# Nine groups, a second copy of the middle stream's sum, a narrow condition product, and layer 2's scores as four row strips

## The chip, the cores and the metric

The kernel runs on one core of one Trainium2 chip. The metric is the device time of one execution in microseconds (us), as the median of several runs. Nothing is split over cores: one core computes all 32 batches.

## The reference

Four transformer-like layers are applied one after the other to `x` (32 batches, 128 tokens, 128 features, float32), with a condition vector `cond` per batch:

```
layer 0: x += g * attn(mod(ln(x)));  16 heads of 64;  x += g * gelu_mlp(mod(ln(x)))
layer 1: x += proj(attn(film(rms(x)))), 1 head of 128;  x += gelu_mlp(film(rms(x)))
layer 2: x += g * attn(mod(ln(x)));  16 heads of 8;  x += g * gelu_mlp(mod(ln(x)))
layer 3: q_exp = where(row_sum(x) == 0, 0, cond)            # per token
         self  = concat(x, q_exp) @ W_self.T + b_self
         for d in 0, 1: A = adj (or transposed)[:, :, :20]  # 11 labels for each edge
             scores = self.Wq . self[:20].Wk + labels' bias, masked; 16 heads of 8, softmax over 20
             out   += heads' outputs
         x = x + relu(out + self)
```

Two facts matter below. In layer 2 each head has only 8 features, so a score product uses few of TensorE's 128 rows. In layer 3 `W_self` is applied to a concatenation whose second half is either zero or the batch's condition vector, the same for all tokens.

## The kernel before

The 32 batches are worked through in 8 groups of 4 (`G = 4`, so a group has T = 512 token columns, one PSUM bank of float32). Each group passes four **streams** of steps: *front* (layer 0's attention, 8 pairs of heads), *mid* (layer 0's MLP and layer 1), *back* (layer 2) and *end* (layer 3). Letters name a stream of one group: A to H the fronts, I to P the mids, Q to X the backs, a to h the ends. `STEPS` (lines 68 to 158) lists each stream's steps; `ORDERS` (line 181 on) holds, for each of the four engines PE, DVE, ACT and POOL, one string of 1357 letters that was written out by a planner: each letter takes the next step of its stream. Every engine works strictly through its own string and waits on semaphores inside the steps, so a wait on PE holds up everything that follows in PE's string. Groups overlap only as the strings interleave them: in the PE string the mid of group g runs beside the front of g+1, the back beside the front of g+2, the end beside the front of g+3. After the last letter H (front of the last group) there remain P, W, X, f, g and h, and the last 18 letters are h alone. A front has 76 steps, a mid 25, a back 51, an end 18.

`Plan` (line 302) deals the eight PSUM banks: it walks through PE's string and gives each result that begins at a step the bank that was freed longest ago. `order_pairs` (line 242) lists which steps of neighbouring groups must stay in order because they share a buffer. One of them is `y2` of a back before `down (1, 1)` of the next mid: both use the single buffer `x1`, which carries layer 1's result to layer 2.

The steps that the change touches:

- `S2` of a back (PE line 1122): layer 2's scores. A batch has 4 strips of 32 rows (`strip(u)`, 4 heads each) and so 4 units u; the unit's bank gets 4 heads x 128 keys. The moving operand `km` is the keys, zero but for one head in each part. Step k takes two units, 2k and 2k+1, that is two strips and two banks; a batch has two such steps. DVE takes the row maximum (line 1442), ACT the exponentials with their sums (932), PE transposes (1138), ACT copies (938), and `V2` multiplies with the values (1148), one step for a batch, in four column strips.
- `sum3`, `self3` of an end (PE lines 1173 to 1177): `sum3` multiplies x3T with ones; DVE makes `qx` of it (1528: the condition where the sum isn't zero); `self3` adds two products, one of x3T and one of `qx`, and DVE adds the bias (1369) to get `sT`.
- `adj` of an end (PE line 1167, DVE 1508): transposes the edge sums that came by the other direction and builds mask and bias.
- `edges` of a back: 12 pieces of the adjacency, converted on ACT (927), multiplied on POOL (786) and summed twice on DVE (1437, 1438); 4 of 20 edges for all 128 tokens, 8 of 16 edges on 80 partitions.

Float32 products appear in the trace as two MATMUL records each, transposes as one.

Of the kernel before, what the change touches and what calls it, by code (L numbers as in the profile page):

```python
# [12 lines left out]
D = 128  # L13
B = 32
G = 4
NG = B // G
# [38 lines left out]
NJ = 2 * G  # L55
# [59 lines left out]
def back_steps():  # L115
    steps = norm_steps(4) + [Step("kq2", 0, ["k2", "q2"], ["k2", "q2"]), Step("v2", 0, ["v2"], ["v2"])]
    for s in range(2 * G + 1):
        for what, lag in (("S2", 0), ("T2", 1), ("T2'", 1), ("E2", 0)):
            w = s - lag
            if not 0 <= w < 2 * G:  # L120
                continue
            begins, ends = {"S2": ([("A", 2 * w), ("A", 2 * w + 1)], [("A", 2 * w)]),
# [11 lines left out]
def end_steps():  # L134
    steps = [Step("adj", 0, ["adj"], ["adj"]), Step("sum3", 0, ["sum3"], ["sum3"]),
             Step("self3", 0, ["self3"], ["self3"]), Step("qk3", 0, ["q3_0", "q3_1", "k3"], ["q3_0", "q3_1", "k3"])]
    for s in range(NU3 + 5):
        begins, ends = [], []
        if s < 2:
            begins.append(f"vb_{s}")  # L140
            ends.append(f"vb_{s}")
        if s in (S4 + 4, NU3 + 4):
            begins.append(f"a3_{s // S4 - 2}")
            ends.append(f"a3_{s // S4 - 2}")
        if 0 <= s - 4 < NU3:
            begins.append(("T3", s - 4))
            ends.append(("T3", s - 4))
        if s < NU3:
# [9 lines left out]
FRONTS, MIDS, BACKS, ENDS = "ABCDEFGH", "IJKLMNOP", "QRSTUVWX", "abcdefgh"  # L158
STEPS = {}
for _g in range(NG):  # L160
    STEPS.update({FRONTS[_g]: front_steps(_g + 1 < NG), MIDS[_g]: mid_steps(), BACKS[_g]: back_steps(), ENDS[_g]: end_steps()})


NPIECES = 12
PIECES = [(0, e, 20) for e in range(0, G * NK3, 20)] + [(1, e, 16) for e in range(0, D, 16)]
EDGE_EVERY = 3


def edge_slot(i):

    return i // EDGE_EVERY - 1 if i % EDGE_EVERY == 0 and i >= EDGE_EVERY else None

EDGE_LAST = EDGE_EVERY * (NPIECES + 2)

# [7 lines left out]
            "AAAAAAAAAAAAAAAAAAAAAAAAAAAAAAAAAAAAAAAAAAAAAAAAAAAAAAAAAAAAAAAAAAABBAAAAAAAAAIBIBBBBBIBBBBBBIBBIBBI"  # L184
            "IBBBIIBBBBBBBBBIBIBIIBIBIBBBBBBBIBBIBBBIIIBBBBBBBBBBBBIBBBIBIBBIBBIBBCCBBBBCCBBCBCQCCBCCQJJCCCCCJCQC"
            "CJJQCCQCQCQJQJQQQQCJQJCQCCQJCCCQCQCCCQQQJQCCCCCQQJQCJCQCQQJCCCQQJCJQCQJQCQCJCQQCCCQQQCCQCJJCQJCQCCCC"
            "QJQQJCCCQCCCJJQCCQCCCQCCQCDCQQDDDDRaDRRDDaRRDaKRRKDaKRRaKaKRKRDRRDKDRRaDDDDRDDDKDDRDRRRKDDRDRRDaDDDR"
            "DaRDDKRKDDDaDKRRDRKRRKDDKRDDDRaDDKDDDRDDDaRKDDKDRRKDDDKDRDRDKDRDaRDDDaDRDKRDKDDDDRKaRDDRRaKRDRDaRREa"
            "EELSELESbEESbESSbSESLSEbSLSLbSSELEbSLESSEEbEEEESELSEEESESESSLEEEEbSELSEESEbSESEELEESbLESEESSLLLSEESS"
            "bEEEEELEEESEbLSESLLESEEESSSEbELEESbLEEEEEEESLLSESbESSEbLELESEbSESESSFbTTMFFFcTMFcTTFFMFcFFTcTTMcMTTT"  # L190
            "TFFFMMTTTcFcFMTFFMFFFTFTTFMFFTTFFcFFTFFFTFcFTTFFTMFFFTTcTFTMMTMMTFFFFTcFFMFFcTFMTFMTFFTMFFFFTFFFFFFT"
            "cFFMTFFMFcTFMTMcTTcTFFFFMFcTMTFFTFTFTTGUGcUGGGGdGdUGNUUGNdUNUdUUNNdUdNUUUUGGNGdUUGGGNUGGGNGUGGNGUGUG"
            "UUGGUGdGGGUGdNGGUGUdNUUGGUUGGNNGGNGUUGdNGUGGNdGUGUGUGGGNGGUGGUUGGUGGNGNGdUGGGGNdUGGGNNUGGdUdUUGGNdUG"
            "GNUGUUUHHdVHGHVVeHVHVeHOOHVeVVVOeVOHOeVHHeHVHHHOVVOHHHeVHHHVVHHeOVVVVOVHeVeVVVOOVVHeOVeVOHeOOHHVHHVH"
            "HVHHeHOVHVHHHHVeVOHHOHVeHVVeHOVOHHHVHHOHHHVHVVOOeHHHHVVOVHHVHHHOHVVHHfWHHHHHfWHWfHWWfPWPWWPffPPWWWfP"
            "WPWWWPPPWWfWWPWWfWPfWPWPfWWfWPPWPWWWPWWfWWPfWWPfPWWWfWfWPWPWWfWPWPWWWWgXXXgXXXXXgXgXXXXgXgXXXXgXXXXX"
            "gXgXXXXXXXXgXXXXXggXXXgXXggXXgXXXgXXXXghhhhhhhhhhhhhhhhhh"),
        "DVE": (
            "AAAAAAAAAAAAAAAAAAAAAAAAAAAAAAAAAAAAAAAAAAAAAAAAAAAAAAAAAAAAAAAAAABAAAAABAAAAAIBBBBIBBIBBBBBBIIBBIBB"
# [1453 lines left out]
```

## Time and profile before

| | |
|---|---|
| median of 3 runs | 1184.86 us (1183.1 to 1186.69) |
| the profiled execution | 1181.46 us |
| its span in the trace | 1179.7 us |
| PE (TensorE) busy | 1085.0 us, 92% of the span, 8411 matmul records |
| DVE (VectorE) busy | 881.7 us, 75% |
| ACT (ScalarE) busy | 770.1 us, 65% |
| POOL (GpSimd) busy | 435.8 us, 37% |
| mean granted TensorE clock | 0.965 of full speed |

```profile
## 2 busy tenths in 40 slices
PE   5898999999999999999999999999989988778675
PEld 4565765776577656676667756766567755546434
DVE  2465767786899687996799788996887678858645
ACT  0655567984788547874789548974678628837712
```

Each digit is the busy share of one fortieth of the span (29.5 us), in tenths; 9 is 90% or more. PEld is TensorE's weight loading, which overlaps the products. In the rows below, a busy time is the time in which at least one instruction of the group ran, a mean is that of one instruction with its latency, and an idle time before a group says whom its engine waited for.

### The profile page before, as it was taken

The numbers are of one execution on the slowest core, as the hardware profiler recorded it, in microseconds if no ns is written. First come the engines' busy times: TensorE is split into PE (matmuls) and PEld (weight loads), VectorE is DVE, ScalarE is ACT, GpSimd is POOL, SyncE is SP. The second block draws the span as 40 slices with busy tenths as digits, with TensorE's granted clock in tenths as the row PEclk, the third lists the DMA queues.
The fourth block names the chain that finished last, engine by engine and source line by source line (L and its number), as shares of the span: only waits on it lengthen the run. The fifth ranks groups of instructions, "written<-read, shape, count | busy, mean of one in ns | idle before, by whom it ended". The sixth has DMA issues, their size and how long they took to land.

```text
span 1179.7 us, 24111 instructions
## 1 busy us (share of the span) xinstructions
PE 1085.0 (92%) x8411; PEld 734.9 (62%) x8411; DVE 881.7 (75%) x2510; ACT 770.1 (65%) x2888; POOL 435.8 (37%) x599
## 2 busy tenths in 40 slices
PE   5898999999999999999999999999989988778675
PEld 4565765776577656676667756766567755546434
DVE  2465767786899687996799788996887678858645
ACT  0655567984788547874789548974678628837712
POOL 1231323431454323542355324541344234515313
PEclk9999999999999989999999999999989999988885
DMA  8000000001000100001000100001000100010000
GB/s 259 2 9 1 11 10 1 10 11 32 1 11 11 32 10 9 2 11 41 1 11 3 39 9 11 2 2 40 1 10 2 41 1 1 2 40 1 1 9 10
DMA packets 21822, 20.98 MB, mean 18 GB/s; under 512 B 1143, under 2 KB 20296, under 8 KB 21448
## 3 DMA queue, kind: packets, MB, share of 16 engines
q1 hardware_dynamic: 18536, 15.26, 4.6%
q10 hardware_dynamic: 3168, 4.19, 1.2%
q8 instruction: 69, 1.13, 0.4%
q14 instruction: 49, 0.40, 0.1%
HBM read 17.35 MB, written 2.10 MB: 16 GB/s over the span
## 4 chain that ended last, share of the span: by engine, by line
PE 68%; DVE 19%; ACT 5%; POOL 4%; issue 3%; DMA 1%; POOLq 0%; DVEq 0%; ACTq 0%
PE bank L1002 11%; PE bank L1021 7%; PE bank L1009 7%; PE bank L1026 5%; PE bank L1047 5%; PE bank L1072 5%; PE bank L1062 5%; PE bank L1056 4%; PE bank L1130 4%; PE bank L1138 3%; PE bank L996 3%; PE bank L1148 2%; PE bank L1220 2%; PE bank L1209 2%; ACT prob_space L932 2%
## 5 line engine op out<-in xcount | busy, mean ns | idle before, releaser
L756 POOL TENSOR_TENSOR fprobs<-fprobs,frinv 128x512 f32<-128x512 f32 x128 | 132.7, 1041 | 249.2 <-DVE frinv L1315 248.3
L932 ACT ACTIVATE prob_space<-bank,negmax 128x128 f32<-128x128 f32 x512 | 181.4, 385 | 34.1 <-DVE negmax L1442 33.9
L868 ACT ACTIVATE fprobs<-bank,fnegmax 128x128 f32<-128x128 f32 x512 | 181.1, 388 | 31.3 <-DVE fnegmax L1310 31.1
L1002 PE MATMUL bank<-fhT,w_qkv 128*128 128x512 f32 x256 | 126.1, 615 | 1.5 <-DVE fv L1324 0.8
L729 POOL TENSOR_TENSOR rstd<-veps,half 128x4 f32<-128x4 f32 x40 | 40.5, 1014 | 208.6 <-DVE veps L1272 173.6
L868 ACT ACTIVATION_READ_ACCUMULATOR fprobs<-bank,fnegmax 128x1 f32 x512 | 116.7, 228 | 0.0
L932 ACT ACTIVATION_READ_ACCUMULATOR prob_space<-bank,negmax 128x1 f32 x512 | 115.7, 226 | 0.0
L1310 DVE TENSOR_REDUCE fnegmax<-bank 128x4 f32<-128x512 f32 x128 | 82.1, 682 | 40.3 <-PE bank L1047 39.8
L1442 DVE TENSOR_REDUCE negmax<-bank 128x4 f32<-128x512 f32 x128 | 82.2, 683 | 22.0 <-PE bank L1130 21.6
L874 ACT ACTIVATE fprobsT<-bank 128x512 f32<-128x512 f32 x128 | 74.5, 605 | 36.5 <-PE bank L1056 36.4
L879 ACT ACTIVATE fk<-bank 128x512 f32<-128x512 f32 x64 | 38.8, 607 | 82.0 <-PE bank L1002 82.0
L1138 PE MATMUL bank<-ident,prob_space 128*128 128x128 f32 x512 | 78.6, 287 | 6.0 <-ACT prob_space L932 5.6
L1056 PE MATMUL bank<-ident,fprobs 128*128 128x128 f32 x512 | 75.8, 279 | 7.6 <-POOL fprobs L756 7.0
L938 ACT ACTIVATE prob_space<-bank 128x512 f32<-128x512 f32 x128 | 76.4, 620 | 8.6 <-PE bank L1138 8.4
L1056 PEld LDWEIGHTS bank<-ident,fprobs 128*128 128x128 f32 x512 | 58.5, 142 | 36.2 <-issue 19.0
L1130 PE MATMUL bank<-km,qk 32*128 32x256 f32 x512 | 75.6, 422 | 3.5 <-POOL km L793 2.2
L1138 PEld LDWEIGHTS bank<-ident,prob_space 128*128 128x128 f32 x512 | 60.6, 147 | 27.3 <-issue 17.6
L1009 PEld LDWEIGHTS bank<-w_qkv,fhT 128*128 128x128 f32 x512 | 65.6, 194 | 19.0 <-issue 16.4
L838 POOL TENSOR_TENSOR p<-p,rinv 128x320 f32<-128x320 f32 x64 | 47.3, 740 | 75.8 <-DVE rinv L1548 75.8
L1047 PE MATMUL bank<-fk,fq 64*128 64x128 f32 x1024 | 74.4, 284 | 0.6 <-issue 0.2
L786 POOL TENSOR_TENSOR adjw<-adjf,labels 80x176 f32<-80x176 f32 (+1 forms) x96 | 53.6, 559 | 54.7 <-ACT adjf L927 54.7
L1047 PEld LDWEIGHTS bank<-fk,fq 64*128 64x128 f32 x1024 | 62.3, 187 | 17.7 <-issue 14.6
(193 smaller groups left out, 2503.6 us busy)
## 6 DMA issues: line engine op xcount, KB each, us to landing
adj<-in_mask_BxSxSx_ik SPq DMA_DIRECT2D x8, 440.0 KB
adj<-in_mask_BxSxSx_ik SPq DMA_DIRECT2D x32, 110.0 KB
x_norm<-in_x SPq DMA_DIRECT2D x8, 256.0 KB, 2.9
x_res<-in_x SPq DMA_DIRECT2D x8, 256.0 KB, 2.8
out<-x_out SPq DMA_DIRECT2D x8, 256.0 KB, 2.3
w_qkv<-in_L_cond_W_qkv ACTq DMA_DIRECT2D x1, 1536.0 KB, 6.9
prob_space<-in_w_mod SPq DMA_DIRECT2D x1, 1024.0 KB
w_up<-in_w_up ACTq DMA_DIRECT2D x1, 768.0 KB, 13.2
```

What stands on the lines that cost most here:

```text
L756: pool.tensor_tensor(p, p, wide(frinv[:, u, :], D), ALU.mult).then_inc(fnormed.sem, 1)
L868: ins = act.activation(fprobs[:, u % NP, b, :], P.bank(("S", u))[:, tok(b)], ACT.Exp, bias=fnegmax[:, u, b:b + 1], accum_out=frsum[:, u, b ...
L932: ins = act.activation(probs[:, u % NP, i, :], P.bank(("A", u))[:, tok(i)], ACT.Exp, bias=negmax[:, u, i:i + 1], accum_out=rsum[:, u, i:i ...
L1002: ins = pe.matmul(P.bank(result)[:, :], w, a, start=(i == 0), stop=(i == len(terms) - 1))
L1009: ins = pe.matmul(P.bank(result)[:, tok(b)], a[:, tok(b)], w, start=(i == 0), stop=(i == len(terms) - 1))
L1021: pe.matmul(P.bank(result)[:, :], w_up[:, l, tok(c)], part.hT[:, :], start=True, stop=True).then_inc(P.full_sem(result), 1)
L1047: ins = pe.matmul(P.bank(("S", 2 * c + r))[:, tok(b)], fq[rows, c % 2, tok(b)], fk[rows, c % 2, tok(b)], start=True, stop=True)
L1056: ins = pe.transpose(P.bank(("T", u))[:, tok(b)], fprobs[:, u % NP, b, :], ident[:, :])
L1130: ins = pe.matmul(P.bank(("A", u))[:, tok(2 * n, 2)], qk[strip(u), 0, tok(b)], flat(km[strip(u), b % 2, 2 * n:2 * n + 2, :]), start=True, ...
L1138: ins = pe.transpose(P.bank(("T", u))[:, tok(i)], probs[:, u % NP, i, :], ident[:, :])
L1310: dve.tensor_reduce(fnegmax[:, u, :], P.bank(("S", u))[:, :].rearrange("p (b k) -> p b k", b=G), AX.X, ALU.max, negate=True).then_inc(fmax ...
L1442: dve.tensor_reduce(negmax[:, u, :], P.bank(("A", u))[:, :].rearrange("p (i k) -> p i k", i=HS), AX.X, ALU.max, negate=True).then_inc(max2 ...
```

## The change

1. **Groups.** `SIZES = (2, 4, 4, 4, 4, 4, 4, 4, 2)` replaces 8 groups of 4. Every instruction that covered 512 columns covers `P.t = n * 128`; per-batch loops run over `P.n`; counts of semaphores are lists by group. The first and the last group have two batches. The adjacency comes in n + 8 pieces, in a small group one at every second step in place of every third.
2. **The orders.** All four strings are new (1483 letters each, fronts A to I, mids J to R, backs S to a, ends b to j). `x1` gets two copies, used in turn, and the order pair on it now ties the back of g to the mid of g+2. In the new PE string 128 letters stand ahead of the first mid (before: 78), the spans of neighbouring fronts overlap by 20 to 63 letters (before: by none to 17), after the last front's last step there remain a mid of 2 batches, backs of 4 and 2 and ends of 4, 4 and 2, and the last 14 letters are j alone, of 2 batches.
3. **The condition product.** `W_self`'s second half is multiplied with the group's condition columns themselves (n columns), in step `adj`; `qx` is then the product's column where the sum isn't zero, and is added on DVE.
4. **Layer 2's scores.** The even S2 step issues the products of all four strips into four banks; the odd one issues nothing on PE.

```diff
 G = 4
-NG = B // G
+SIZES = (2, 4, 4, 4, 4, 4, 4, 4, 2)
+NG = len(SIZES)
...
-            begins, ends = {"S2": ([("A", 2 * w), ("A", 2 * w + 1)], [("A", 2 * w)]),
+            begins, ends = {"S2": ([("A", 2 * w + j) for j in range(S4)] if w % 2 == 0 else [], [("A", 2 * w)]),
...
-PIECES = [(0, e, 20) for e in range(0, G * NK3, 20)] + [(1, e, 16) for e in range(0, D, 16)]
-EDGE_EVERY = 3
+PIECES = [[(0, e, 20) for e in range(0, n * NK3, 20)] + [(1, e, 16) for e in range(0, D, 16)] for n in SIZES]
+EDGE_EVERY = [3 if n == G else 2 for n in SIZES]
...
-        pairs.append((step_at(b, "y2"), step_at(m2, "down", (1, 1))))
+        if g + 2 < NG:
+            pairs.append((step_at(b, "y2"), step_at(MIDS[g + 2], "down", (1, 1))))
...
-        x1 = sb("x1", [D, G, D])
+        x1 = sb("x1", [D, 2, G, D])
...
                     elif what == "S2":
-                        b = k // 2
                         if k % 2 == 0:
+                            b, units = k // 2, range(2 * k, 2 * k + S4)
                             pe.wait_ge(*km_ready.nth(g, b))
-                        banks_free(P, drained=["q2"] if k == 0 else [], empty=[("A", u) for u in (2 * k, 2 * k + 1)])
-                        for n in range(2):
-                            for u in (2 * k, 2 * k + 1):
+                            banks_free(P, drained=["q2"] if k == 0 else [], empty=[("A", u) for u in units])
+                            for n in range(2):
+                                for u in units:
...
                     if what == "adj":
-                            ins = pe.transpose(P.bank("adj")[:, i * G * NK3:(i + 1) * G * NK3], edge1[:, i, :], ident[0:G * NK3, 0:G * NK3])
+                            pe.transpose(P.bank("adj")[:, i * ne:(i + 1) * ne], edge1[0:ne, i, :], ident[0:ne, 0:ne])
+                        ins = pe.matmul(P.bank("adj")[:, 2 * ne:2 * ne + P.n], w3[:, 1, :], condT[:, 1, P.base:P.base + P.n], start=True, stop=True)
...
-                        linear(P, "self3", [(w3[:, 0, :], x3T[:, :]), (w3[:, 1, :], qx)], after=["sum3"])
+                        linear(P, "self3", [(w3[:, 0, :], x3T[:, :])])
...
                     if what == "adj":
-                        dve.tensor_copy(gcond[:, :], condT[:, 1, bass.ds(g * G, G)]).then_inc(chain.sem, 1)
-                        dve.wait_ge(*chain.last(g))
                         dve.wait_ge(*P.full("adj"))
+                        dve.tensor_copy(gcond[:, 0:P.n], P.bank("adj")[:, 2 * ne:2 * ne + P.n])
...
                     elif what == "self3":
-                        biased(P, "self3", sT[:, :], ROW["L3_cond_b_self"])
+                        c = ROW["L3_cond_b_self"]
+                        dve.wait_ge(*P.drained("sum3"))
+                        dve.wait_ge(*P.full("self3"))
+                        dve.scalar_tensor_tensor(sT[:, 0:P.t], P.result("self3"), col[:, c:c + 1], qx[:, 0:P.t], ALU.add,
+                                                 ALU.add).then_inc(P.free_sem("self3"), 1)
```

## Rows read from the trace of the kernel before

**Rows 1.** Windows: stretch, us, busy of PE PEld DVE ACT POOL, PEclk, DMA, GB/s.
```profile
12.00:66.00 54.00, 49.19 (x310) 35.36 (x311) 25.07 (x68) 25.19 (x99) 14.26 (x16) 1.00 0.29 77
200.00:943.80 743.80, 726.40 (x5829) 496.89 (x5828) 603.81 (x1713) 539.34 (x2065) 294.68 (x398) 0.99 0.05 14
...
958.30:1050.00 91.70, 75.36 (x610) 49.73 (x608) 72.33 (x218) 58.80 (x207) 36.19 (x55) 1.00 0.05 14
1050.00:1134.00 84.00, 66.65 (x495) 43.01 (x496) 58.03 (x163) 50.28 (x189) 29.85 (x50) 0.82 0.00 1
1134.00:1179.70 45.70, 26.56 (x186) 16.93 (x185) 25.94 (x60) 9.26 (x18) 16.04 (x28) 0.69 0.04 12
```

**Rows 2.** A slice in the middle: all engines, then L1130 alone (PE, PEld).
```profile
589.90:648.80 58.90, 57.73 (x539) 42.52 (x538) 53.82 (x147) 50.79 (x215) 30.52 (x39) 1.00 0.03 7
...
589.90:648.80 58.90, 5.66 (x40) 3.41 (x40) 1.00 0.03 7
```

**Rows 3.** Timeline of PE, merged: start, us, line, tiles, records.
```profile
195.73 1.05 PE L1009 MATMUL bank<-w_qkv,fhT 128*128 128x128 f32 x8
196.62 1.06 PE L1009 MATMUL bank<-w_l,hT 128*128 128x128 f32 x8
197.61 1.09 PE L1062 MATMUL bank<-fprobsT,fv 128*64 128x128 f32 x16
198.63 1.13 PE L1130 MATMUL bank<-km,qk 32*128 32x256 f32 x8
199.69 1.98 PE L1026 MATMUL bank<-mhid,w_down 128*128 128x512 f32 x4
...
210.62 1.16 PE L1047 MATMUL bank<-fk,fq 64*128 64x128 f32 x16
211.71 1.12 PE L1072 MATMUL bank<-fattnT,w_out 128*128 128x512 f32 x2
...
213.77 1.08 PE L1148 MATMUL bank<-prob_space,vm 128*32 128x128 f32 x32
214.78 1.09 PE L1062 MATMUL bank<-fprobsT,fv 128*64 128x128 f32 x16
```

**Rows 4.** Groups by line and form: busy us in total, mean ns, idle before.
```profile
L1442 DVE TENSOR_REDUCE negmax<-bank 128x4 f32<-128x512 f32 x128 | 82.2, 683 | 22.0 <-PE bank L1130 21.6
...
L1130 PE MATMUL bank<-km,qk 32*128 32x256 f32 x512 | 75.6, 422 | 3.5 <-POOL km L793 2.2 <-ACT fk L879 1.2
...
L1324 DVE COPY fv<-bank 128x512 f32<-128x512 f32 x64 | 43.6, 681 | 10.4 <-PE bank L1009 10.1
...
L1437 DVE TENSOR_REDUCE edge<-adjf 80x16 f32<-80x176 f32 x64 | 20.3, 317 | 0.3
...
L1463 DVE COPY vm<-bank 128x128 f32<-128x128 f32 x32 | 7.0, 277 | 1.2 <-PE bank L1009 1.0
...
L1170 PE MATMUL bank<-ident,edge 80*128 80x80 f32 x16 | 2.5, 236 | 0.0
```

**Rows 5.** The chain of waits: exponentials and their sums for two units.
```profile
1013.26 2.76 ACT prob_space L932 x16
```

**Rows 6.** Timeline of the tail, first PE, then DVE.
```profile
1133.77 1.12 PE L1002 MATMUL bank<-x3T,ones 128*128 128x512 f32 x2 [0.80 <-DVEq L1498]
1136.68 1.12 PE L1002 MATMUL bank<-x3T,w 128*128 128x512 f32 x2 [1.78 <-DVE q L1528]
1137.64 1.02 PE L1002 MATMUL bank<-q,w 128*128 128x512 f32 x2
...
1151.92 1.08 PE L1209 MATMUL bank<-ident,p 128*80 128x128 f32 x4 [4.75 <-POOL p L838]
...
1170.23 1.08 PE L1209 MATMUL bank<-ident,p 128*80 128x128 f32 x4 [0.74 <-POOL p L838]
...
1135.50 1.12 DVE L1528 TENSOR_SCALAR q<-bank,gcond 128x128 f32<-128x128 f32 x4
1138.70 0.75 DVE L1369 TENSOR_SCALAR sT<-bank,col 128x512 f32<-128x512 f32 x1 [2.08 <-PE bank L1002]
```

More of the change, by code:

```diff
@@ L15 @@
 G = 4
-NG = B // G
+SIZES = (2, 4, 4, 4, 4, 4, 4, 4, 2)
+NG = len(SIZES)
+BASE = [sum(SIZES[:g]) for g in range(NG + 1)]
+assert BASE[NG] == B
 T = G * D
@@ L343, in bank, with result @@
         return self.plan.banks.ps[self.number(r)]
+    def result(self, r):
+        return self.bank(r)[:, 0:self.t]
     def full_sem(self, r):
@@ L522, in build @@
         adj1 = sb("adj1", [G * NK3, D * L3], I32)
-        PW = max(n for _, _, n in PIECES) * L3
+        PW = max(n for some in PIECES for _, _, n in some) * L3
         adjf = sb("adjf", [D, 2, PW])
@@ L578, in build, with batches, halves, units2 @@
         x_stored = sem("x_stored")
+        def batches(n):
+            return n
+        def halves(n):
+            return n // 2
+        def units2(n):
+            return S4 * n
+        def units3(n):
+            return S4 * n // 2
+        def pieces(n):
+            return n + D // 16
+        def end_links(n):
+            return END_LINKS + units3(n)
         fmod_ready = count("fmod_ready", 1)
@@ L638, in run @@
             for letters, stream in ((FRONTS, front), (MIDS, mid), (BACKS, back), (ENDS, last)):
-                streams.update({letter: stream(plan.view(letter), g) for g, letter in enumerate(letters)})
+                streams.update({letter: stream(plan.view(letter, g), g) for g, letter in enumerate(letters)})
             weave(plan.orders["DVE" if name == "SP" else name], streams)
@@ L800, in back @@
                         head_keys(0)
-                    elif what == "S2" and k % 2 == 0 and k // 2 + 1 < G:
+                    elif what == "S2" and k % 2 == 0 and k // 2 + 1 < P.n:
                         head_keys(k // 2 + 1)
@@ L897, in biased @@
                 act.wait_ge(*P.full(use))
-                act.activation(dst, P.bank(use)[:, :], ACT.Identity, bias=col[:, b:b + 1]).then_inc(P.free_sem(use), 1)
+                act.activation(dst[:, 0:P.t], P.result(use), ACT.Identity, bias=col[:, b:b + 1]).then_inc(P.free_sem(use), 1)
             def mid(P, g):
@@ L1243, in prologue @@
                 pe.wait_ge(*fz_ready.nth(0, 0))
-                for b in range(G):
+                for b in range(SIZES[0]):
                     ins = pe.transpose(ps[4][:, tok(b)], fz[:, b, :], ident[:, :])
@@ L1258, in statistics @@
             def statistics(chain, g, i, src, k):
-                for b in range(G):
+                n = SIZES[g]
+                for b in range(n):
                     ins = dve.bn_stats(stats[:, i, b, :], src[:, b, :])
@@ L1263, in statistics @@
                 dve.memset(held[:, 0:1], 0.0)
-                for b in range(G):
+                for b in range(n):
                     ins = dve.bn_aggr(mv[:, i, b, :], stats[:, i, b, :])
@@ L1498, in back @@
                         dve.sem_inc(x3_ready.sem, 1)
-                    if edge_slot(i) is not None:
-                        edges(edge_slot(i) - 2)
+                    if edge_slot(g, i) is not None:
+                        edges(edge_slot(g, i) - 2)
                     yield
-                assert BACK.chain.n == BACK.chain.per, BACK.chain.n
+                assert BACK.chain.n == BACK.chain.per[g], BACK.chain.n
             def last(P, g):
@@ L1576, in last @@
                     yield
-                assert chain.n == chain.per, chain.n
             def prologue():
```

481 lines of the change are left out of this document (244 added, 237 removed).

## The prediction

> **What bounds the kernel now.** I read the page's table of busy times first: PE is busy for 1085.0 of the span's 1179.7 us, DVE for 881.7, ACT for 770.1. So PE's own work is the bound, with 94.7 us in which it idles. Then the windows, to see where those lie [rows 1]: from 200 to 943.8 us PE idles for 743.8 - 726.40 = 17.4 us only, at a full clock, while in the 221.4 us after the last front (958.3 to the end) it idles for 16.3 + 17.4 + 19.1 = 52.8 us. There the granted clock is also down, to 0.82 and 0.69 of full, so some of the stretches run at 1.2 in place of 2.4 GHz. That leaves 94.7 - 17.4 - 52.8 = 24.5 us, 9 to 12 of them before the first product. Two kinds of change can pay: less PE work in the middle, where each us of it is nearly a us of the span, and less tail. What can spoil it is DVE, which in single slices of the middle is nearly as full as PE (53.82 of 58.9 us, [rows 2]).
>
> **Layer 2's scores.** Before, an S2 step is 8 records of 256 columns, and PE's next work starts 199.69 - 198.63 = 1.06 us after it began [rows 3]. A batch has two such steps, 16 records, 2.12 us; 32 batches have 512 records, of 75.6 us busy [rows 4], 2.36 us a batch with the slow-clock stretches in it. What do four strips cost? The trace has no product with four row strips into four banks, so I bound it. From above: four strips go no faster than two, 2.12 us a batch, nothing saved. From below: four at a time take as long as two, half of the 75.6 us is saved, 37.8. The nearest rows are the tiled products that are there [rows 3]. Two row strips (L1047): 16 records of 128 columns in 211.71 - 210.62 = 1.09 us. Two column strips (L1062): 16 in 198.63 - 197.61 = 1.02. Four column strips (L1148): 32 in 214.78 - 213.77 = 1.01. The whole array (L1009): 8 in 196.62 - 195.73 = 0.89. So a step costs eight rounds of 0.11 us plus 0.12 to 0.20 for the change of tiling, whether one, two or four run in a round. Row strips load 128 columns of weights where column strips load 32, but in the two-strip steps that doesn't show. I take the full effect at the undisturbed pace: 16 records in the 1.06 us of today's 8. Saved: 32 x 1.06 = **33.9 us** (range 0 to 37.8).
>
> The Trainium skill, "TensorE: Matmul & The Clock Gate", section "Measured speedup vs the span model", has 3.07x for four row tiles where four would be ideal. An estimate by that figure: a batch takes 4 x 1.06 / 3.07 = 1.38 us in place of 2.12, and 23.6 us are saved instead of 33.9. No row of this trace shows four row strips, so it can't be said here which is right; the four column strips of L1148 show no such loss.
>
> What the edit adds is a wait: PE now needs four empty banks at once, and everything in PE's string stands behind that wait. The units drain one after the other: DVE 0.68 us each [rows 4], ACT 2.76 us for two [rows 5], 5.5 for the batch. The third and fourth bank are so held about 2.8 us longer than when their products were issued by a step of their own. I worked both PE strings through `Plan`'s rule: before, a bank is taken again at the earliest 3 letters after its last use ended, on average 6.5 for these scores; after, at the earliest 1, on average 5.5. A letter is 1179.7 / 1357 = 0.87 us, so room is tighter, but the average is still near 5 us. I put this into the middle's idle time, below.
>
> **The condition product.** Removed from PE: 8 times two records of 512 columns. In the tail they start at 1137.64, after x3T's at 1136.68 [rows 6], so 0.96 us a step: -7.6 us. Added: 9 times two narrow records; the nearest row is the transposes of 80 columns in the same step, 2.5 / 16 = 0.16 us each [rows 4]: +2.8. Also, PE no longer waits for `qx`: in the last group x3T's product waits 1.78 us for it [rows 6]. What is late next is DVE's sT, which needs `qx` (done at 1135.50 + 1.12 = 1136.6) as well: it can start at about 1136.7 and not at 1138.70, -2.0 us. Its operation now reads a third operand; 0.75 us may become 1, hidden everywhere but in the last group. DVE's new wait in front of sT is for its own last instruction, with nothing behind it that is ready sooner. Sum: **-6.8 us** (range -11 to 0, the last if the waits were covered).
>
> **Nine groups: fixed costs.** Work per batch stays. What comes on top is one more set of instructions whose cost doesn't shrink with the columns. On PE that is the change of tiling: 8 score steps at 1.09 - 0.89 = 0.20 and 8 value steps at 1.02 - 0.89 = 0.13 [rows 3], 2.6 us, and about as much again in steps that become too short to hide weight loads: **+5 us**. On DVE a copy of 512 columns takes 681 ns and one of 128 takes 277 [rows 4], so 142 ns are fixed; about 100 such instructions a group give 14 us, and the 8 pieces of the adjacency on 80 partitions, which a half group has in full, 16 x 0.317 = 5.1. DVE goes to about 901 us. That is beside PE's work unless DVE bounds (upper end for this item: +25).
>
> **The tail.** The stretch after the last front holds P, W, X, f, g and h. Afterwards it holds a mid of 2, backs of 4 and 2, ends of 4, 4 and 2 batches. The work that leaves it isn't saved, it is done in the middle; what is saved is idle time and slow clock. I go by the three windows [rows 1]. Last window, one end alone: 45.7 us, 26.56 busy, 19.1 idle. With two batches it has 4 units instead of 8. The first T3 comes 18 us into it (1151.92) and the last starts at 1170.23, so 8 units take 18.3 + 1; 4 units fewer save some 10 us, and the shorter operations ahead of them and behind them 5 more. Half of its 26.56 us of work, 13, only moves to the middle, so 2 of that is real gain; half of its slow-clock loss (26.56 us at a clock of 0.69 are some 20 at the full one) is 3 more. The middle window, a back with an end (84.0 us, clock 0.82): half of the back leaves; its chains of norms stay as long, and I give 2 for the clock. The first window (16.3 idle): with half a mid and three streams in it, a quarter of the idle time goes, 4. And the first window's back is no longer issued from a string in which x1 must be free: the stretch around the last front gets work of two neighbours; 4 more, by analogy with 200 to 943.8. Sum **-15 us** (range -30, if nearly all of the idle share went, to 0).
>
> **The start.** A alone has 49.19 of 54 us busy [rows 1]. With two batches each step is half as long, the chain from scores over maximum, exponentials and POOL's product to the transposes less than half as short: more idle by a few us; the smaller loads (x, the adjacency) give back one. **+2 us** (-3 to +8).
>
> **The middle.** PE loses 34 of its some 726 us there and gains the tail's work; DVE rises from 603.8 / 743.8 = 81% to about 86%, and bank room is tighter. Idle time is 17.4 us now; I take **+6** (range -10, since fronts of neighbours may now overlap and the second x1 unties backs from mids, to +40).
>
> **Sum**, against the profiled execution: 1179.7 - 33.9 - 6.8 + 5 - 15 + 2 + 6 = 1137.0 us of span. The execution has 1181.46 - 1179.7 = 1.76 us around it: 1138.8. The median of the runs is 1184.86 - 1181.46 = 3.4 above this execution: **1142 us**, 3.6% less than before.
>
> **Rivals.**
>
> *The strips don't run four at a time* (the write into four banks or four weight loads of 128 columns take turns). For it: S2's row strips are nowhere more than two now. Against: the even cost of two and four column strips [rows 3]. All of the 33.9 us stay: 1142 + 34 = 1176.
>
> *DVE bounds the phases of layer 2.* In the slice of [rows 2] DVE has 53.82 of 58.9 us; PE's S2 is 5.66 us in it, and half of that can't be taken out when DVE has 5.1 us left and gets 2.5 us more of its own. About every second slice of the middle is like this, with 1.5 to 3 us lost each in some 7 of them, 11 us: 1153. For it: DVE waits for PE there no more than 1.1 us a slice on S2's account (21.6 us in all, [rows 4]). Against: the new orders spread fronts and backs over each other.
>
> *More comes out of the orders than out of the work.* With fronts that overlap by 20 to 63 letters the rest of the 24.5 us, the idle time of the middle and the tail fall together: another 20 us, 1122. For it: PE idle after 958 is 24% of the stretch. Against: only chains of norms and the softmax of an end are left there.
>
> *Slower: four empty banks at once stall PE.* All of PE stands behind the wait. If in a batch the fourth bank comes late by the drain of two units, 2.76 us [rows 5], PE loses 32 x 2.76 = 88 us instead of the 6: 1142 + 82 = 1224. It decides from (42.7 + 6) / 32 = 1.5 us of stall a batch on: there the whole gain is gone. For it: the closest take is 1 letter after the release. Against: on average 5.5 letters, and PE has other streams' steps between.
>
> The Trainium skill, "TensorEngine Tiling (Array Packing)", "Performance Considerations" and "Gotcha 1: PSUM Pressure", speaks for these last two: after a tiling speedup the PSUM copy may be the bottleneck, and row tiling takes more banks. The trace shows the copies' side of it: DVE's maximum of 0.683 and ACT's 1.38 us a unit against a new 0.27 us of PE.
>
> **How the numbers follow.** Forecast (1130 to 1158 as its own range) 0.48; DVE bound near 1153 0.18; more from the orders near 1122 0.16; strips two at a time near 1176 0.10; bank stalls above 1185 0.08. The forecast and its two neighbours hold 0.82; to leave out no more than 2 in 10 the range goes from 1108 to 1172. A measurement of this kernel can tell about 0.3%, 3.6 us. Faster than 1181.3: all but the stalls and a little of the strips' case, 0.89; within 0.3%: 0.03; slower: 0.08.
>
> **What would show it.** Right: records of L1130's successor still 512, but about 38 to 42 us busy in total and a pitch near 1.06 us for 16; L1002's q,w group gone; PE busy near 1045 us; idle time after the last front near 30 us, the last stretch of one end under 32 us. Wrong: a step of 16 records that takes 1.4 to 2.1 us (strips); waits of scores and transposes for ACT's prob_space that total over 20 us (banks); DVE over 90% in the middle with PE waiting for its results (DVE); PE's idle time from 200 us to the last front over 40 us would make the forecast too low.

## The result and the profile after

The changed kernel takes **1179.7 us** (median of 12 runs, 1176.7 to 1183.61) against 1183.51 for the kernel before (12 runs). The ratio is 0.9966, with a 95% interval of 0.995 to 0.9983: a gain of 0.2 to 0.5%, where 3.6% were forecast. The time lies above the predicted range (1108 to 1172).

The page of the changed kernel: span, busy times, the busy tenths in 40 slices, and the shares of the chain that ended last.

```profile
span 1179.8 us, 24614 instructions
PE 1062.1 (90%) x8525; PEld 738.2 (63%) x8525; DVE 898.0 (76%) x2623; ACT 807.8 (68%) x2956; POOL 444.5 (38%) x632
...
PE   5999999999999989999999989998899879867774
PEld 4667767766666666567675657666675655555453
DVE  2657668778787897788887888878868885984874
ACT  2666668768977678767876776776875876774552
...
PE 56%; DVE 22%; ACT 14%; POOL 3%; issue 3%; DMA 1%; SPq 0%; POOLq 0%; DVEq 0%; ACTq 0%
```

PE's busy time fell by 1085.0 - 1062.1 = 22.9 us, and its idle time rose by 117.7 - 94.7 = 23.0. The span is the same to 0.1 us. DVE has 16.3 us more than before, ACT 37.7.

Three windows of it, in the columns of [rows 1]: the middle, all that comes after the last front's last step (now at 1007.7), and the last end by itself.

```profile
200.00:943.80 743.80, 703.14 (x5765) 482.51 (x5768) 606.09 (x1761) 554.06 (x2041) 295.52 (x408) 0.99 0.05 13
1007.70:1179.80 172.10, 120.65 (x998) 86.11 (x997) 122.30 (x335) 92.33 (x321) 63.56 (x112) 0.81 0.03 7
1151.80:1179.80 28.00, 12.10 (x100) 7.92 (x99) 14.12 (x36) 5.97 (x11) 7.68 (x14) 0.65 0.05 15
```

The first answers to the second row of [rows 1]: PE now idles for 743.8 - 703.14 = 40.7 us there, before 17.4. After the last front it idles for 172.1 - 120.65 = 51.5 us, before 52.8. The last end alone takes 28.0 us, before 1179.7 - 1133.8 = 45.9. The rest of the balance: 0 to 200 us 23.5 before and 16.5 now; 943.8 to the last front's end 1.0 before and 9.1 now. So the idle time came back where PE had been nearly full. Counted from 200 us to the last front's end it is 807.7 - 757.96 = 49.7 us, before 758.3 - 739.94 = 18.4. The mean granted clock after the last front is 0.81, before 0.87, so slow-clock time was not won back there either.

Groups of instructions, one for each shape, in the columns of [rows 4]. L1163 is the successor of L1130, L1479 of L1442; L1206 is the narrow condition product that took the place of L1002's `q,w` group (9.1 us busy).

```profile
L1479 DVE TENSOR_REDUCE negmax<-bank 128x4 f32<-128x512 f32 x128 | 81.9, 680 | 12.3 <-PE bank L1163 11.6
L1163 PE MATMUL bank<-km,qk 32*128 32x256 f32 x512 | 38.5, 415 | 10.4 <-ACT prob_space L969 2.8 <-ACT fprobs L899 2.1 <-DVE vm L1500 1.2
L1206 PE MATMUL bank<-condT,w 128*128 128x4 f32 x14 | 2.3, 232 | 0.0
```

Layer 2's scores are down from 75.6 to 38.5 us, with the same 512 records. The idle time before them rose from 3.5 to 10.4. PE's timeline shows one step of them, to be held against [rows 3]:

```profile
376.10 1.15 PE L1163 MATMUL bank<-km,qk 32*128 32x256 f32 x16
377.17 1.09 PE L1094 MATMUL bank<-fprobsT,fv 128*64 128x128 f32 x16
```

Sixteen records, and the next work starts 377.17 - 376.10 = 1.07 us later; before, eight records took 1.06. Four row strips into four banks do run four at a time.

The waits of PE (who is waited for: us in total, times, longest), the largest and that of the scores for their banks:

```profile
PE bank L1245 <- POOL p L869: 11.6, 8, 5.9
PE bank L1269 <- ACT prob_space L885: 9.2, 1, 9.2
PE bank L1027 <- DVE z L1317: 8.5, 4, 3.0
PE bank L1088 <- POOL fprobs L786: 6.0, 12, 1.4
PE bank L1178 <- ACT prob_space L969: 6.0, 3, 3.9
PE bank L1171 <- ACT prob_space L963: 5.9, 6, 2.0
...
PE bank L1163 <- ACT prob_space L969: 2.8, 2, 2.1
```

The 9.2 us are PE's wait for its first operands and were there before (9.2). None of the others is large. The added idle time is not one new wait. It is spread over many, most of 0.3 to 3 us, in front of nearly every kind of step.

### The profile page after: what moved, and what is told of

It reads as the page before. It is cut to its first block, busy times and chain, and to the rows that moved or that the text cites. A ratio compares the mean times of both kernels' runs of the same rounds, so it can differ in the third digit from the quotient of the medians.

```text
span 1179.8 us, 24614 instructions
## 1 busy us (share of the span) xinstructions
PE 1062.1 (90%) x8525; PEld 738.2 (63%) x8525; DVE 898.0 (76%) x2623; ACT 807.8 (68%) x2956; POOL 444.5 (38%) x632
## 4 chain that ended last, share of the span: by engine, by line
PE 56%; DVE 22%; ACT 14%; POOL 3%; issue 3%; DMA 1%; SPq 0%; POOLq 0%; DVEq 0%; ACTq 0%
PE bank L1033 9%; PE bank L1041 7%; PE bank L1053 5%; PE bank L1079 5%; PE bank L1058 4%; ACT prob_space L963 4%; ACT fprobs L899 4%; PE bank L1088 4%; PE bank L1094 4%; PE bank L1104 3%; DVE negmax L1479 3%; PE bank L1027 3%; PE bank L1181 2%; DVE p L1605 2%; PE bank L1163 2%
## 5 line engine op out<-in xcount | busy, mean ns | idle before, releaser
L786 POOL TENSOR_TENSOR fprobs<-fprobs,frinv 128x512 f32<-128x512 f32 (+1 forms) x144 | 136.4, 950 | 265.9 <-DVE frinv L1352 265.0
L1033 PE MATMUL bank<-fhT,w_qkv 128*128 128x512 f32 (+1 forms) x288 | 127.7, 564 | 1.1 <-ACT prob_space L963 0.4
L1347 DVE TENSOR_REDUCE fnegmax<-bank 128x4 f32<-128x512 f32 (+1 forms) x144 | 84.0, 624 | 46.5 <-PE bank L1079 46.2
L899 ACT ACTIVATION_READ_ACCUMULATOR fprobs<-bank,fnegmax 128x1 f32 x512 | 111.8, 219 | 0.0
L759 POOL TENSOR_TENSOR rstd<-veps,half 128x4 f32<-128x4 f32 (+1 forms) x45 | 42.5, 945 | 154.2 <-DVE veps L1309 122.3
L905 ACT ACTIVATE fprobsT<-bank 128x512 f32<-128x512 f32 (+1 forms) x144 | 76.3, 557 | 33.4 <-PE bank L1088 33.1
L1479 DVE TENSOR_REDUCE negmax<-bank 128x4 f32<-128x512 f32 x128 | 81.9, 680 | 12.3 <-PE bank L1163 11.6
L1088 PE MATMUL bank<-ident,fprobs 128*128 128x128 f32 x512 | 78.3, 281 | 10.1 <-POOL fprobs L786 6.0
L910 ACT ACTIVATE fk<-bank 128x512 f32<-128x512 f32 (+1 forms) x72 | 40.2, 558 | 62.0 <-PE bank L1033 61.8
L1079 PE MATMUL bank<-fk,fq 64*128 64x128 f32 x1024 | 77.8, 289 | 2.3 <-ACT fk L910 0.7
L1033 PEld LDWEIGHTS bank<-fhT,w_qkv 128*128 128x128 f32 x288 | 51.0, 195 | 41.0 <-issue 31.1
L1094 PE MATMUL bank<-fprobsT,fv 128*64 128x128 f32 x1024 | 71.8, 280 | 3.1 <-issue 1.7
```

What stands on the lines that cost most here:

```text
L786: pool.tensor_tensor(p, p, wide(frinv[:, u, 0:P.n], D), ALU.mult).then_inc(fnormed.sem, 1)
L899: ins = act.activation(fprobs[:, u % NP, b, :], P.bank(("S", u))[:, tok(b)], ACT.Exp, bias=fnegmax[:, u, b:b + 1], accum_out=frsum[:, u, b ...
L905: act.activation(flat(fprobsT[:, u % NP, 0:P.n, :]), P.result(("T", u)), ACT.Copy).then_inc(P.free_sem(("T", u)), 1)
L1033: ins = pe.matmul(P.result(result), w, a[:, 0:P.t], start=(i == 0), stop=(i == len(terms) - 1))
L1079: ins = pe.matmul(P.bank(("S", 2 * c + r))[:, tok(b)], fq[rows, c % 2, tok(b)], fk[rows, c % 2, tok(b)], start=True, stop=True)
L1088: ins = pe.transpose(P.bank(("T", u))[:, tok(b)], fprobs[:, u % NP, b, :], ident[:, :])
```

## The experiments

Three explanations were open at the start. **A**: each part gives what the prediction says when put alone into the kernel before, and nine groups took it back. **B**: the middle is not bound by PE's work; the engines' written-out orders tie the four strings together, and PE's saved time comes back as short waits. **C**: ACT pays, by the loads of its function tables, of which there are 57 in place of 38.

**e1: only the four strips, in the kernel before, with its old orders.** The scores' step of even k begins all four banks and issues what two steps issued; the odd one issues nothing.

```diff
-            begins, ends = {"S2": ([("A", 2 * w), ("A", 2 * w + 1)], [("A", 2 * w)]),
+            begins, ends = {"S2": ([("A", 2 * w + j) for j in range(S4)] if w % 2 == 0 else [], [("A", 2 * w)]),
...
+                            b, units = k // 2, range(2 * k, 2 * k + S4)
+                            banks_free(P, drained=["q2"] if k == 0 else [], empty=[("A", u) for u in units])
```

> The kernel before, its groups and its orders, with layer 2's scores as four strips into four banks and nothing else. Theory A (the four strips pay, the new groups and orders give it back): PE work falls by 34 to 37 us, most of it is in the middle, where PE idled for 17.4 of 743.8 us; 1183.5 falls by 15 to 30 us, to 1153 to 1168. Theory B (four empty banks at once stall PE, so the strips themselves are worth nothing): 1178 or more, with waits before the scores in the trace.

Measured: 1227.43 us, ratio 1.0378 (1.0342 to 1.0414). That is 44 us *slower*. The page, the middle window and the scores' row of e1:

```profile
span 1221.6 us, 24105 instructions
PE 1068.3 (87%) x8411; PEld 720.1 (59%) x8411; DVE 882.2 (72%) x2510; ACT 773.7 (63%) x2888; POOL 435.3 (36%) x599
```

```profile
200.00:943.80 743.80, 673.39 (x5522) 456.44 (x5522) 576.89 (x1635) 515.08 (x1970) 283.04 (x385) 0.99 0.04 12
```

```profile
L1131 PE MATMUL bank<-km,qk 32*128 32x256 f32 x512 | 39.0, 419 | 21.4 <-DVE fq L1321 4.8 <-ACT prob_space L932 4.4 <-ACT fk L879 2.8
```

The product is as cheap as in the changed kernel (39.0 us), and PE is idle for 70.4 us in the middle. The scores' own waits are 21.4 us in the whole execution, the rest stands in front of other steps. A bank begun earlier shifts which bank later results are dealt: by `Plan`'s rule 938 of the 1311 results get another bank than before, and the old orders were written for the other dealing. Which of these costs the time is not shown. Explanation A falls here.

**e2: only the narrow condition product.** `q,w` of 512 columns goes, four columns against `condT` come, and DVE adds them in `sT`.

```diff
+                        ins = pe.matmul(P.bank("adj")[:, 2 * G * NK3:2 * G * NK3 + G], w3[:, 1, :], condT[:, 1, g * G:(g + 1) * G], start=True, stop=True)
...
-                        linear(P, "self3", [(w3[:, 0, :], x3T[:, :]), (w3[:, 1, :], qx)], after=["sum3"])
+                        linear(P, "self3", [(w3[:, 0, :], x3T[:, :])])
...
```

> The kernel before with the narrow condition product alone. My step: 6.8 us less, 1176.7; if the other engines' pace decides, under 3 us less.

Measured: 1178.22 us, ratio 0.9951 (0.9928 to 0.9974), 5.8 us less. The term was -6.8.

**e3: both**, the two edits above together.

```diff
+            begins, ends = {"S2": ([("A", 2 * w + j) for j in range(S4)] if w % 2 == 0 else [], [("A", 2 * w)]),
...
+                        linear(P, "self3", [(w3[:, 0, :], x3T[:, :])])
```

> The kernel before with both, in the old 8 groups and old orders. Theory A: 1145 to 1162, clearly under the changed kernel's 1179.7; what is between is the price of nine groups and their orders. Theory B: 1175 to 1180, the same as the changed kernel.

Measured: 1226.33 us, ratio 1.0372 (1.0335 to 1.0409). The strips' loss stays, and beside them the narrow product is worth only 1.1 us.

**e4: the changed kernel with two strips a step again**, its own orders kept: the lines of e1's diff the other way round.

```diff
-            begins, ends = {"S2": ([("A", 2 * w + j) for j in range(S4)] if w % 2 == 0 else [], [("A", 2 * w)]),
+            begins, ends = {"S2": ([("A", 2 * w), ("A", 2 * w + 1)], [("A", 2 * w)]),
```

> The changed kernel with its scores again two strips at a step, all else of the change kept, its orders too. Theory A: slower than the changed kernel by 20 to 35 us, 1200 to 1215, as PE gets its 34 us back. Theory B (PE is no longer what decides; ACT and DVE do): slower by under 12 us.

Measured: 1218.37 us, ratio 1.0303 (1.0267 to 1.034). Its page:

```profile
span 1219.4 us, 24646 instructions
PE 1107.6 (91%) x8525; PEld 771.3 (63%) x8525; DVE 896.9 (74%) x2623; ACT 810.7 (66%) x2956; POOL 445.6 (37%) x632
```

So one edit costs 44 us in one set of orders and is worth 1218.4 - 1179.7 = 38.7 in the other. Neither figure is the price of the strips. Each string of orders runs the work it was written for clearly better than the other work. Room in the banks is not what decides: by `Plan`'s rule a bank is taken again 6.9 letters after its last use in e4, on average over all results, and 6.3 in the changed kernel, which is the faster of the two.

**e5 and e6: PE's work alone, banks and orders untouched.** e5 is the kernel before without half of the scores' columns (it leaves out half of layer 2's scores); e6 is the changed kernel with each product of the scores issued twice.

```diff
 e5
-                        for n in range(2):
+                        for n in range(1):
...
 e6
-                            for n in range(2):
+                            for t in range(4):
+                                n = t % 2
...
```

> The kernel before, with two strips a step and its old orders and banks, but only the first half of each unit's scores is computed (2 of 4 heads' columns): layer 2's scores cost PE some 1.26 us a batch in place of 2.12 and no bank is taken otherwise than before. Theory A' (PE's work is worth its price, what cost 44 us in the kernel before with four strips is only that banks are taken four at a time in an order that wasn't made for it): 1155 to 1165, 20 to 27 us less. Theory C (the old orders are so tightly set between four engines that less PE work gives little): 1172 or more.

> The changed kernel with four strips and four banks, the products issued twice (same result): PE's scores cost 2.12 us a batch again, 34 us in all, and banks are dealt as in the changed kernel. Theory A': 1179.7 + 30 or more, 1207 to 1215, so that the slower run with two strips at a step (1218) is PE's work. Theory C (PE has room now): 1179.7 + 10 to 20; the rest of the 38 us of the run with two strips is then its changed banks.

Measured: e5 1173.36 us, ratio 0.9923 (0.9893 to 0.9952), 10 us less; e6 1196.48 us, ratio 1.0126 (1.0098 to 1.0153), 16.8 us more than the changed kernel. PE's timelines of the two, one step of each with what follows it:

```profile
198.49 0.70 PE L1130 MATMUL bank<-km,qk 32*128 32x256 f32 x4
199.12 1.99 PE L1026 MATMUL bank<-mhid,w_down 128*128 128x512 f32 x4
```

```profile
380.16 2.01 PE L1164 MATMUL bank<-km,qk 32*128 32x256 f32 x32
382.10 1.09 PE L1094 MATMUL bank<-fprobsT,fv 128*64 128x128 f32 x16
```

A step of e5 takes 0.63 us in place of 1.06, 64 times: 27.5 us less work, and 10.1 / 27.5 = 0.37 us of the time for each us of it. A step of e6 takes 1.94 in place of 1.07, 32 times: 27.8 us more, and 16.8 / 27.8 = 0.60. The prediction had put "nearly a us" there. At 0.37 to 0.60 the strips' 33.9 us are worth 13 to 20.

Not all of the rest came back as waits. All that comes after the last front, in the kernel before, in e5 and in e4 (one fence each, in the columns of [rows 1]):

```profile
958.30:1179.70 221.40, 168.57 (x1290) 109.67 (x1288) 156.30 (x441) 118.33 (x413) 82.07 (x133) 0.87 0.03 9
```

```profile
947.00:1172.10 225.10, 173.12 (x1226) 110.95 (x1224) 156.95 (x441) 118.65 (x413) 81.70 (x133) 0.80 0.03 9
```

```profile
1026.40:1219.40 193.00, 141.29 (x998) 100.27 (x997) 119.70 (x335) 92.78 (x321) 63.84 (x112) 0.75 0.02 7
```

Up to the last front e5 gains 958.3 - 947.0 = 11.3 us with 192 of the 256 records that it lacks, some 0.55 us for each us of work (an estimate: 192 / 256 of the 27.5). After it, with 64 records less, it is 3.7 us longer: PE idles no more than before, but it is busy for 4.6 us more at a mean granted clock of 0.80, before 0.87. In e4 that stretch is 20.9 us longer than the changed kernel's 172.1, more than half of e4's loss, with the same idle time (51.7 and 51.5 us) at a clock of 0.75 against 0.81; 11.1 us of it are the scores. The clock belongs to the runs and not only to the profiled ones: its median over an execution is 0.952 in e5's runs and 0.959 in those of the kernel before beside them (0.965 in its profiled execution, so the traces overstate the difference). A part of what less PE work should give thus goes with the clock of the tail; no run holds the clock fixed, and its share stays open.

Held against e1 and e4, the two runs also price the moved banks: much the same PE work with every bank as it was is worth 10 us less (e5) and 17 more (e6), with products moved to other steps and the banks dealt anew it read as 44 more (e1, less work) and 39 more (e4, more work).

**e7 and e8: all table loads but the first two gone**, by Identity in place of Gelu (the gelu is left out), in the changed kernel and in the one before.

```diff
-                    act.activation(part.hid[:, c, 0:P.t], P.result(f"f{l}_{c}"), ACT.Gelu,
+                    act.activation(part.hid[:, c, 0:P.t], P.result(f"f{l}_{c}"), ACT.Identity,
```

> The changed kernel with Identity in place of Gelu in all three MLPs: ACT loads no table any more (57 loads of 1.283 us, 73 us, in its trace). If the loads, 19 more than before, are what takes the gain: 20 to 40 us less than 1179.7, and clearly more than the same edit gives in the kernel before. If not: under 10 us less.

> The kernel before with Identity in place of Gelu: 38 loads, 49 us of ACT, go. If ACT has slack everywhere but in the tail: 3 to 8 us less than 1183.5. If loads matter as much here as in the changed kernel, both fall alike and the extra loads explain nothing.

Measured: e7 1175.45 us (0.9939, 0.9915 to 0.9963), 4 us below the changed kernel; e8 1182.55 us (1.0005, 0.9979 to 1.0031), no change. The loads in the changed kernel:

```profile
L924 ACT ACT_TABLE_LOAD x28 | 35.9, 1283 | 0.5
L899 ACT ACT_TABLE_LOAD x21 | 26.9, 1283 | 0.4
L1009 ACT ACT_TABLE_LOAD x6 | 7.7, 1283 | 0.1
L963 ACT ACT_TABLE_LOAD x2 | 2.6, 1283 | 0.0
```

They are 73.1 us of ACT (48.8 before), and the 55 of them that e7 does without are worth 4 us. Explanation C is a small term.

**r1 to r4: the same work, orders written anew.** Explanation B says that a fitting order is what is missing. Only the four strings of `ORDERS` differ: single steps were moved past their neighbours on one engine or on all, within the kernel's own rules (`order_faults`, `Plan`), wherever the traces' durations and waits let one expect a shorter chain. PE's steps stand 1.8 to 2.1 letters from their old place on average, ACT's 2.9 to 3.5.

```diff
 ORDERS = {
     "all": {
         "PE": (
-            "AAAA...BBBABAABBBABAAABBBBABABBBABBBBBBBBA"
+            (as many letters of each kind, in another order; DVE, ACT and POOL likewise)
```

> The kernel before with its own work and banks rule, only the four engines' orders of steps written anew (neighbouring steps exchanged where the measured durations of the traces say that a wait shrinks). It is the control for the other three. If what e1 to e5 showed is that the orders and not the engines' work set the time, an order is worth tens of us in either direction, and this runs at 1140 to 1165. If the old orders were as good as orders get (the rest being PE's 1085 us of busy time), it stays within 10 us of 1184.

> The kernel of e3 (eight groups, four strips, narrow condition product: 1226 with the old orders), orders written anew in the same way. Theory A (the gain of the four strips was lost in the orders written down for it): far below e3, at 1130 to 1155, and below the changed kernel's 1180 and below r1 by 8 to 15 us. Theory B (four banks taken at once cost what the strips save, whatever the order): at or above r1, 1165 to 1185. Theory C (nothing to gain from orders): 1180 or more.

> The changed kernel (nine groups), orders written anew. Theory A: 1135 to 1160, some 25 to 40 below the changed kernel. By the price of the ninth group (PE busy other than scores and the condition product rose by some 20 us) it stands 3 to 8 us above r2. If nine groups pay by their shorter tail (221 to 172 us from the last front step to the end) it stands 5 to 15 us below r2. Theory C: within 5 us of 1180.

> Nine groups with two strips a step again (e4: 1218 with the changed kernel's orders), orders written anew for it. Against r3 it is the price of the four strips by themselves when each side has orders of its own: if PE's work is what is bought, 17 to 35 us above r3; if 1 us of PE work is worth 0.4 to 0.5 us in these strings, 10 to 18 above; if four banks at once cost what the strips save, within 5 of r3.

| | work | old orders | written anew | ratio to before, 95% |
|---|---|---|---|---|
| r1 | the kernel before | 1183.5 | 1168.45 | 0.9843 to 0.9894 |
| r2 | e3: eight groups, strips, narrow product | 1226.3 | 1144.02 | 0.9645 to 0.9702 |
| r3 | the changed kernel | 1179.7 | 1144.80 | 0.9642 to 0.9696 |
| r4 | e4: nine groups, two strips | 1218.4 | 1143.88 | 0.9652 to 0.9696 |

All four fall, e3's work by 82 us. r2, r3 and r4 beat both kernels, near the 1142 us that were forecast. That is no late proof of the sum: r4 gets there without the four strips, and the kernel before falls too when its orders are rewritten, so r3 is 24 us faster than r1 and not 43. The pages of r3 and of r4:

```profile
span 1139.3 us, 24635 instructions
PE 1039.4 (91%) x8525; PEld 728.9 (64%) x8525; DVE 896.9 (79%) x2623; ACT 804.2 (71%) x2954; POOL 445.6 (39%) x632
```

```profile
span 1142.6 us, 24632 instructions
PE 1065.3 (93%) x8525; PEld 749.3 (66%) x8525; DVE 892.7 (78%) x2623; ACT 802.8 (70%) x2954; POOL 446.6 (39%) x632
```

r4 has 1065.3 - 1039.4 = 25.9 us more PE work than r3 and takes no longer; PE idles for 99.9 us in r3 and for 77.3 in r4. When each side has its own orders, the four strips buy nothing with nine groups: their time is turned into waits. Whether four banks at once or the other engines' strings make these waits is not settled. A tighter dealing of banks is not what the changed kernel lost its time to, for r3 has the same one (on average 6.3 to 6.4 letters from use to use in both) and takes 35 us less. In r3's middle window and in its scores' row the waits are still there:

```profile
200.00:943.80 743.80, 708.41 (x6000) 494.83 (x5999) 631.31 (x1831) 571.87 (x2122) 308.35 (x427) 1.00 0.05 14
```

```profile
L1163 PE MATMUL bank<-km,qk 32*128 32x256 f32 x512 | 38.5, 416 | 13.6 <-DVE p L1602 8.2 <-ACT prob_space L969 2.2 <-issue 0.8
```

6000 PE records fit into the window where the changed kernel has 5765, with DVE at 631.31 us instead of 606.09. The scores wait for DVE's `p` of an end, a step of another stream.

**s1 to s4: how much of that is the writing?** r1 and r2 lie 24 us apart, more than the strips' work explains. s1, s3 and s4 are second, independent writings for the work of r1, r2 and r3; s2 is e2's work (two strips, narrow product) with orders of its own.

The edits are e2's and the strings of `ORDERS` in s2, and the strings of `ORDERS` alone in s1, s3 and s4.

> The kernel before with a second, independent writing of its orders. It tells how far two writings of the same method differ: r1 was 1168. If the scatter of the writing is what separates r1 from r2 (24 us), this comes out near 1150; if the two-strip kernel of eight groups really stands behind, within 6 us of 1168.

> Eight groups, two strips, the narrow condition product, orders written anew: it splits the 24 us between r1 and r2. If the four strips are what r2 has of it, 1158 to 1165 (only the 5 to 7 us of the narrow product below r1). If the strips are worth nothing once orders fit, as r3 against r4 says, 1140 to 1150.

> The work of r2 with a second writing of the orders. Within 5 us of r2's 1144 if the method settles on one value, up to 12 above it if it doesn't.

> The work of the changed kernel with a second writing of the orders. Within 5 us of r3's 1145 if the method settles on one value; if it reaches 1138 or less, nine groups are ahead of eight by their shorter tail.

Measured: s1 1155.66 us (ratio 0.9794, 0.9744 to 0.9845), s2 1162.1 (0.984, 0.9801 to 0.9879), s3 1159.97 (0.9819, 0.9772 to 0.9867), s4 1145.89 (0.9705, 0.9664 to 0.9746). The kernel before took 1178.92 us beside these four, 5 less than beside r1 to r4, so the ratios are what compares. With eight groups two writings of one and the same work lie 0.0075 (r1, s1) and 0.0145 (r2, s3) apart, 9 and 17 us. s2 lands where its expectation put strips that pay, 1158 to 1165, but s3, which has the four strips as well, is only 2 us faster than s2, and s1, which has neither the strips nor the narrow product, is 6 us faster. So the strips and the narrow product can't be priced there: both expectations for s2 assumed a sharper instrument than this is. With nine groups the two writings lie 0.0036 apart (r3, s4), some 4 us, and the three kernels of nine groups lie within 4 us of the best one of eight (r2) and some 10 us or more below the four others. Set against the same number of writings of the old work, the change is worth 24 us (r3 against r1) and 10 (s4 against s1).

## Why the prediction was wrong

By its own steps:

- **Layer 2's scores, -33.9 (range to 37.8).** The price on PE was right: 1.07 us for 16 records, 37.1 us less busy in the group's row. What it was worth in time was not (see the middle). The estimate by the Trainium skill, "TensorE: Matmul & The Clock Gate", section "Measured speedup vs the span model", was 1.38 us a batch; the trace doesn't agree. From two strips to four the busy time goes down by 75.6 / 38.5 = 1.96. The rival "not four at a time" is out.
- **The condition product, -6.8.** The size is right: e2 measured -5.8. That it came by the priced steps is not shown, for PE is busy for 1084.8 us in e2's trace, before for 1085.0. In the changed kernel its wait of 1.78 us is gone from the tail; `sT` starts 1153.89 - 1151.81 = 2.1 us after the stretch's first product, where it was 1138.70 - 1133.77 = 4.9 [rows 6], a part of that because the last group is half as large.
- **Nine groups' fixed cost, +5.** Its size can't be read from the changed kernel, where the other PE groups grew by some 20 us. With rewritten orders PE is busy for 1039.4 us with nine groups (r3) and 1040.8 with eight (r2):

```profile
span 1141.8 us, 24103 instructions
PE 1040.8 (91%) x8411; PEld 710.1 (62%) x8411; DVE 879.1 (77%) x2510; ACT 769.6 (67%) x2888; POOL 436.1 (38%) x599
```

  So the fixed cost is not above a few us, and the 20 us go with the orders. What they are is not shown; the slow-clock stretches are likely one part (mean clock 0.961 in the changed kernel's profiled execution, 0.975 in r3's). The same instructions are busy for 1085.0 us in the kernel before, at a mean clock of 0.965, and for 1072.8 in r1, at 0.956:

```profile
span 1166.1 us, 24120 instructions
PE 1072.8 (92%) x8411; PEld 733.4 (63%) x8411; DVE 885.6 (76%) x2510; ACT 768.4 (66%) x2888; POOL 435.8 (37%) x599
```

  The sum for the fixed cost took 0.12 to 0.20 us for a change of tiling, against a whole-array step of 0.89 us. The next whole-array step of [rows 3], with a tiled one behind it, takes 197.61 - 196.62 = 0.99, so that price isn't a clean reading. On DVE the forecast of 901 us was met (898.0). ACT's added work, 37.7 us, was not priced at all; by e7 its table loads are a small part of the miss.
- **The tail, -15.** The last end was right, 17.9 us shorter for some 15, most of it work that moved. The sum's 15 us were to be idle time and slow clock, and of these next to nothing came: PE idles for 51.5 us after the last front, before for 52.8, and the mean clock there is 0.81, before 0.87. The steps of the last end, PE's timeline:

```profile
1151.81 0.70 PE L1033 MATMUL bank<-x3T,ones 128*128 128x256 f32 x2
1152.35 0.59 PE L1033 MATMUL bank<-x3T,w 128*128 128x256 f32 x2
...
1165.28 1.07 PE L1245 MATMUL bank<-ident,p 128*80 128x128 f32 x4 [5.94 <-POOL p L869]
...
1171.36 1.07 PE L1245 MATMUL bank<-ident,p 128*80 128x128 f32 x4 [1.28 <-POOL p L869]
```

  Against [rows 6], the first unit's wait for POOL's `p` grew from 4.75 to 5.94 us, and four units take 6.1 us where eight took 18.3. Ahead of that end, from 1007.7 to 1151.8, PE idles for 35.5 us, and in the matching stretch before for 33.7.
- **The start, +2.** Wrong in sign: PE's idle time from 12 to 66 us went from 4.8 down to 2.5, and from 0 to 200 us from 23.5 to 16.5.
- **The middle, +6. This is the step that failed**, with the sentence under it, that each us of PE work in the middle is nearly a us of the span. PE's idle time rose there by 23.3 us in place of 6, and PE's busy time outside the scores didn't stay what it was, as said above. e5 and e6 measured 0.37 and 0.60 us for each us of PE work, without moving any step. The prediction's own last sign of being too optimistic came true as well: over 40 us of idle time from 200 us to the last front, where 49.7 were measured. I had read a PE that idles for 2% as a PE that bounds. What the runs fit is this: PE was full because the orders handed to the four engines had been fitted to that work, each with fixed places for the steps of four streams. By this reading, whoever makes one string shorter lets a next step in it meet an operand or a bank that isn't there yet. That orders decide is shown (r3 has the changed kernel's work and takes 35 us less); which string holds which step up was not traced.
- **The rivals.** "DVE bounds": as worded it is out in the changed kernel (606.09 of 743.8 us, 81%), though 26 us less PE work buy nothing in r3 against r4, and DVE may be a part of that. "Four empty banks stall PE": PE waits 10.4 us at the scores, not 88; but in e1 the same edit with unfitted orders costs 44 us, the size of this rival's loss by another way, for only 21.4 us of the waits stand at the scores. "More from the orders", 1122: the orders held a real reserve, which those of the changed kernel leave unused. r3 takes 35 us of it and comes to 1145, not to 1122.

The sum, reassembled: the span was to fall by 42.7 us and didn't. By the prediction's own sign PE's busy time was to come near 1045 us, 40 less, and came to 1062.1 (17 off); the idle time was to fall by the other 3 and rose by 23.0 (26 off). Of its cause it is shown that orders alone are worth 35 us for the changed kernel's work, and 82 for e3's. Three things stay open: how the loss divides between waits and the clock of the tail; what each part is worth in a kernel with perfect orders, for the scatter of the writings with eight groups is larger than the parts; and which engine's string bounds r3.

## What to carry to other kernels

Where every engine runs a written-out order of steps of several streams, an engine that is 98% busy need not be the one whose work sets the time. Here a us of its work was worth 0.37 to 0.60 us, so run a kernel with the same places and less work before a saved us is priced. Look at the granted clock of the tail too: it can take back what the middle gave. An edit that moves steps or changes which bank a result gets is tested only together with orders of its own; with those of the other kernel the same edit read as +44 and as -39 us. Rewrite the orders of the kernel before as well, for otherwise their gain is put down to the edit. Compare two independent writings before a difference between two orders is given to the edit.

## What the runs showed of the hardware

- Four row strips of 32 rows into four banks run side by side: 16 records of 256 columns take 1.07 us, as long as eight of two strips (1.06).
- A step of 32 such records (e6) takes 1.94 us and one of four (e5) 0.63, where 8 of two strips and 16 of four take 1.06 and 1.07: by an estimate from these figures some 0.2 us of a step don't depend on its records.
- A table load of ACT takes 1.283 us, 57 of them 73.1 us; with 55 taken away the kernel was 4 us faster.
- The busy time of PE is not a constant of its instructions: 8525 records were busy for 1062.1 us in the changed kernel, 1043.3 in s4 and 1039.4 in r3.
- Fewer records needn't mean less busy time: after the last front PE was busy for 168.57 us with 1290 records at a mean granted clock of 0.87 (the kernel before), and for 173.12 with 1226 at 0.80 (e5).
